# A transformer pair on one core: the spread expert weights are multiplied in on GpSimd instead of VectorE

## Chip, core and metric

One core of one Trainium2 chip. The metric is the device time of one execution, in microseconds (us): the median of several runs. TensorE is the matrix engine (PE; its weight loads are PEld), VectorE is DVE, ScalarE is ACT, GpSimd is POOL, and SyncE (SP) issues nearly all DMAs.

## What is computed

Two transformer layers on x of 4 batches x 512 tokens x 128 features, all float32. Layer 0 is cross attention with 16 heads on a context of 154 rows and a layer of 8 experts of width 512, of which each token uses two. Layer 1 is a masked self attention, a cross attention and a feed-forward with layer norms between them, and then a second expert layer: 32 experts of width 64, of which a router picks six for each token, and a shared expert. This last part is what the change touches. Cut to what matters:

```python
def expert_step(acc, inp):
    gu, dn, c = inp                       # c: this expert's weight for every token
    g = xf @ gu[:I].T
    u = xf @ gu[I:].T
    o = jax.nn.silu(g) * u @ dn.T
    return (acc + c[:, None] * o, None)
routed, _ = jax.lax.scan(expert_step, zeros, (experts_gate_up, experts_down, combine.T))
sh = silu(xf @ shared_gate_w.T) * (xf @ shared_up_w.T)
out = x + routed + sh @ shared_down_w.T
```

The kernel multiplies by c ahead of the down product: (c * silu(g) * u) @ dn, which is the same sum.

## The kernel before

**Tiling.** A batch is one unit of 512 tokens. Features or hidden units lie on the 128 partitions and the 512 tokens on the free axis, so that nearly every instruction of the expert layers is 128x512. In the second expert layer two experts of width 64 fill 128 rows; with the shared expert that makes ND = 17 pairs, n = 0 to 16, n = 0 the shared one. For each pair TensorE makes a gate product into PSUM bank 0 and an up product into bank 1 (`gates`, each by `product3`, three matmuls of split operands, L1493 to L1495), and later a down product (`downs`, L1851, float32, two instructions in the trace), which adds all pairs up in bank 2. Banks 0 and 1 are single: the next gate product waits until ScalarE has read bank 0, the next up product until VectorE has read bank 1.

**Between them** stand, for each pair: ScalarE's silu of bank 0 into `s32` (L1002), VectorE's multiplication of it by bank 1 into one of four buffers of `h32` (L1445, "silu times up"), and for n = 1 to 16 a second VectorE multiplication in place, by a tile of `CB` (L1451). `CB` holds the two experts' weights for all 512 tokens, spread over the 64 partitions of each: the router's weights go to DRAM and come back row by row (`spread_second` on SP, L711, two DMAs for each pair, four slots). A slot is loaded anew when the multiplication that read it is done (`d_h`). A buffer of `h32` is written anew when the down product four pairs before is done (`d_dn`). At the end of a batch ScalarE copies bank 2, TensorE turns it back, VectorE adds it to x (L1459) and SP stores it (L716).

**What else runs beside it.** GpSimd has: for every layer norm an addition (L424) and a power (L427) between VectorE's steps (`Norm`, L395 to L418), the accumulation of the first expert layer (`stage_b`, L776), the addition norm2b (L786), and `split1` (L748), which makes the low half of the second layer's weights out of pieces `raw1`. There are five of these; piece 0 is the shared expert and pieces 1 to 4 serve pairs 1 to 4, 5 to 8, 9 to 12 and 13 to 16. VectorE has the steps of all norms, the attention's maxima and normalisations (L1269 to L1320), the affine steps (L1252, L1255), the split of xT (L1190, L1193) and the router (L1388 to L1431).

**Order.** Every engine works through one list. Each stage is a generator that yields ahead of each step, and `merged` (L75) interleaves the stages of all batches by due times: tables at the head of the file (`PLAN_SP`, `PLAN_POOL`, `PLAN_ACT`, `PLAN_DVE`, `PLAN_PE`) give one number for each step of each batch, and the step with the lowest goes next. The tables come from a planner. On the chip only the order counts: an engine waits for semaphores and for nothing else, and a step that waits holds up all behind it on its engine. The stages overlap over batches: while the second expert layer of batch 0 runs, the attention of batch 3 does, and the router of the next batch runs beside the second expert layer of the one before. Only the second expert layer of batch 3 has nothing beside it.

Of the kernel before, what the change touches and what calls it, by code (L numbers as in the profile page):

```python
# [91 lines left out]
class Signal:  # L92
# [7 lines left out]
    def then(self):  # L100
# [7 lines left out]
    "constants": [[6, 1272, 10975]],  # L108
    "load_x": [[0], [1040], [2704], [5590]],
    "load_context": [[1260], [4711], [7811]],  # L110
    "second_weights": [[14389, 14395, 28061, 38108, 39646, 41268]],
    "load_context1": [[14407], [24876], [31482], [35078]],
    "store": [[48439], [50521], [56182], [57613]],
    "spread_first": [[13617, 13859, 14401, 14945, 15567, 16098, 16858, 17511, 18133], [18975, 19217, 19342, 20142,
        21401, 22143, 23263, 23892, 24870], [26203, 26446, 26452, 27125, 28055, 28944, 30116, 30829, 31476], [32967,
        33210, 33216, 33959, 35072, 35774, 37822, 38062, 38535]],
    "spread_second": [[37816, 38084, 38096, 38541, 38553, 40408, 40666, 41025, 41256, 41444, 41808, 42078, 42388,
# [7 lines left out]
    "norm_a": [[710, 737], [1818, 1845], [3788, 3815], [7460, 7487]],  # L125
    "values": [[1946], [5119], [8117], [11089]],
    "key_tails": [[1983, 3916], [4316, 5058], [8157, 8218], [9729, 11027]],
    "norm_b": [[6000, 6027], [13177, 13204], [18984, 19787], [26163, 26191]],
    "stage_b": [[14945, 15567, 16098, 16858, 17511, 18133, 18858, 19342], [21045, 21401, 22143, 23263, 24803, 24939,
        25480, 26037], [27645, 28055, 28944, 30116, 32053, 32189, 32389, 32873], [34455, 35593, 35774, 36972, 38062,  # L130
        39028, 39269, 40028]],
    "split1": [[24731, 39396, 39671, 40659, 43013]],
    "stage_c": [[19770, 19888, 23766, 23793, 24603, 24630, 25242, 26614, 26642], [26486, 26513, 30945, 30972, 31922,
        31949, 33420, 33790, 33818], [33289, 33316, 36714, 36741, 38426, 38453, 38899, 40154, 40181], [40531, 40558,
        43780, 43807, 45949, 45976, 46745, 48033, 48060]],
    "norm_d": [[30641, 30668], [35461, 35489], [44684, 44712], [49438, 49465]],
# [3 lines left out]
    "split0": [[2783, 3508, 4085, 4134, 4183, 8886, 8935, 8984]],  # L140
    "prepare_a": [[1174], [2939], [5666], [8837]],
    "query_stacks": [[1729, 2105, 2714, 3732], [4391, 5152, 6048, 6659], [7500, 8169, 8735, 9348], [10184, 11142,
        11545, 12352]],
    "key_stacks": [[1500, 1535, 1569, 1604, 1642, 1677, 1778, 1813], [3438, 3473, 4232, 4267, 4904, 4939, 4974, 5009],
        [7143, 7178, 7265, 7300, 7851, 7939, 7974, 8008], [9523, 9558, 9645, 9680, 10873, 10908, 10943, 10978]],
    "group": [[2322, 2429, 2478, 2543, 2593, 2665, 3001], [2890, 3055, 3107, 3259, 3311, 3383, 3634], [3683, 3797,
# [6 lines left out]
    "output": [[5390], [8462], [11308], [14105]],  # L153
    "prepare_b": [[11973, 12537, 13553], [16155, 16980, 18911], [22407, 25236, 26140], [29424, 30188, 32904]],
    "base": [[14692], [20981], [27582], [34392]],
    "gelus": [[13862, 14049, 14159, 14228, 14478, 14633, 14787, 14942, 15100, 15341, 15409, 15611, 15769, 16095, 16207,
# [9 lines left out]
    "stage_c": [[18671, 19695, 20323, 20406, 20426, 20692, 20870, 21031], [27096, 27118, 27139, 27160, 27470, 28555],  # L166
        [33978, 34000, 34021, 34042, 34340, 35280], [40073, 40096, 41062, 41083, 41372, 42859]],
    "exps_c": [[21080, 21246, 21729, 21918], [27694, 27863, 28301, 28489], [34538, 34708, 35353, 35542], [41767, 41939,
        42341, 42529]],
    "moves_c": [[21706, 21983, 22203, 22355], [28604, 29180, 29381, 29514], [35329, 35607, 35827, 36020], [42136,  # L170
        42595, 42820, 43004]],
    "cross": [[22785, 23326, 23495, 23534, 23573, 23932, 25395], [29958, 30331, 30370, 30409, 30448, 30908, 32556],
        [36796, 37218, 37387, 37426, 37465, 37804, 39112], [43715, 44458, 44627, 44666, 44705, 45054, 47035]],
    "prepare_d": [[34947, 36069, 37753], [40444, 41985, 44926], [46139, 46320, 49178], [51071, 51475, 53224]],
# [1766 lines left out]
```

## Time and profile before

| | |
|---|---|
| runs | 597.2 us median of 3 (596.64 to 597.66) |
| profiled execution | 596.67 us, of which the span of the trace is 594.9 us |
| mean granted TensorE clock | 0.997 of full |
| busy, share of the span | PE 96%, PEld 63%, DVE 68%, ACT 54%, POOL 18% |
| first down product of the second expert layer | 415.6 us, last 589.5 us |
| chain that ended last | PE 80%, DVE 10%, ACT 4%, issue 2%, POOL 2% |

A busy PE is modelled from pipelined matmuls, so that 96% busy is not 96% of what the array could do. The granted clock is the share of TensorE's full 2.4 GHz that the chip allowed. The chain of waits goes back from the last instruction, at each step to what released it. "POOL x <- DVE y" in a view of waits reads: GpSimd's instruction that writes x sat waiting for VectorE's that writes y.

### The profile page before, as it was taken

Reading aid. Unit: us, or ns where it says so; the run is one execution under the profiler, and the core shown is the slowest. Engines: PE = TensorE matmul, PEld = TensorE weight load, DVE = VectorE, ACT = ScalarE, POOL = GpSimd, SP = SyncE. Lnnn points to the kernel's source line nnn. Section 1 sums busy time; section 2 is a strip of 40 time slices with the busy share of each in tenths; the row PEclk is TensorE's granted clock in tenths of the full one; section 3 lists DMA queues with packets and bytes.
Section 4 is the critical chain, followed back from the end, with each engine's and each line's share of the span. In section 5 each row is a group of like instructions: output and inputs, shape, how many; then the busy total and the mean of one; then the engine's idle time right before and its main releaser. Section 6 shows DMA issues by size and latency. Waiting matters only on the chain.

```text
span 594.9 us, 8098 instructions
## 1 busy us (share of the span) xinstructions
PE 569.7 (96%) x2512; PEld 374.7 (63%) x2512; DVE 401.7 (68%) x1265; ACT 322.5 (54%) x566; POOL 105.4 (18%) x120
## 2 busy tenths in 40 slices
PE   4899999999999999999999899999899999999997
PEld 3556666665566667656676466666666676666664
DVE  6888989774132344666637585777889999768564
ACT  1587688766454476644855348745292542342321
POOL 3111110000111311242202432126201110100000
PEclk9999999999999999999999999999899999999999
DMA  4400000300311100101111011061321233341431
GB/s 119 195 15 10 18 10 2 105 39 19 107 36 35 54 20 19 36 28 54 60 31 44 14 42 44 1 199 39 122 75 51 90 119 98 111 138 62 143 120 56
DMA packets 23306, 38.35 MB, mean 64 GB/s; under 512 B 3776, under 2 KB 9536, under 8 KB 22880
## 3 DMA queue, kind: packets, MB, share of 16 engines
q1 hardware_dynamic: 22832, 37.44, 19.9%
q8 instruction: 20, 0.33, 0.2%
q10 hardware_dynamic: 432, 0.40, 0.2%
q14 instruction: 22, 0.18, 0.1%
HBM read 36.45 MB, written 1.38 MB: 64 GB/s over the span
## 4 chain that ended last, share of the span: by engine, by line
PE 80%; DVE 10%; ACT 4%; issue 2%; POOL 2%; DMA 1%; DVEq 0%; POOLq 0%; ACTq 0%
PE ps L1681 16%; PE ps L1493 9%; PE ps L1495 9%; PE ps L1851 9%; PE ps L1494 9%; PE ps L1488 3%; PE ps L1568 3%; PE ps L1588 3%; PE ps L1500 3%; PE ps L1603 2%; PE ps L1600 2%; PE ps L1758 1%; PE ps L1738 1%; DVE NM L1156 1%; PE ps L1530 1%
## 5 line engine op out<-in xcount | busy, mean ns | idle before, releaser
L1493 PE MATMUL ps<-xThi,w1s 128*128 128x512 f32 x256 | 147.5, 576 | 2.9 <-DVE h L1445 2.6
L911 ACT ACTIVATE h<-ps,early 128x512 f32<-128x512 f32 x128 | 86.7, 687 | 88.8 <-PE ps L1495 68.9
L1681 PE MATMUL ps<-h,w2s 128*128 128x512 f32 x256 | 122.5, 594 | 3.3 <-DVE ty L1245 3.2
L1495 PE MATMUL ps<-xTlo,w1s 128*128 128x512 f32 x256 | 101.4, 396 | 0.0
L1494 PE MATMUL ps<-xThi,w1s 128*128 128x512 f32 x256 | 100.9, 394 | 0.0
L1002 ACT ACTIVATE s<-ps 128x512 f32<-128x512 f32 x68 | 40.7, 598 | 95.4 <-PE ps L1495 93.8
L1493 PEld LDWEIGHTS ps<-xThi,w1s 128*128 128x128 f32 x256 | 48.5, 190 | 37.3 <-issue 18.2
L1681 PEld LDWEIGHTS ps<-h,w2s 128*128 128x128 f32 x256 | 46.2, 189 | 35.5 <-issue 23.8
L1494 PEld LDWEIGHTS ps<-xThi,w1s 128*128 128x128 f32 x256 | 48.7, 190 | 28.6 <-issue 24.3
L776 POOL TENSOR_TENSOR acc_o<-acc_o,ty 128x512 f32<-128x512 f32 x32 | 41.9, 1310 | 140.2 <-DVE ty L1245 115.7
L1445 DVE TENSOR_TENSOR h<-s,ps 128x512 f32<-128x512 f32 x68 | 46.5, 684 | 28.2 <-PE ps L1495 21.0
L1851 PE MATMUL ps<-h,w2s 128*128 128x512 f32 x128 | 63.5, 592 | 0.0
L1156 DVE TENSOR_REDUCE NM<-ps 128x2 f32<-128x308 f32 x128 | 56.1, 471 | 10.5 <-PE ps L1568 9.2
L1245 DVE TENSOR_TENSOR ty<-ps,WB 128x512 f32<-128x512 f32 x32 | 22.0, 686 | 53.4 <-PE ps L1681 53.4
L1495 PEld LDWEIGHTS ps<-xTlo,w1s 128*128 128x128 f32 x256 | 48.3, 189 | 11.2
L1451 DVE TENSOR_TENSOR h<-h,CB 128x512 f32<-128x512 f32 x64 | 44.2, 690 | 1.0
L1568 PE MATMUL ps<-KS,QS 128*128 128x320 f32 x128 | 41.8, 375 | 2.2 <-DVE NM L1156 1.4
L864 ACT ACTIVATE h<-ps 128x512 f32<-128x512 f32 x54 | 31.1, 597 | 10.8 <-PE ps L1588 9.7
L1568 PEld LDWEIGHTS ps<-KS,QS 128*128 128x128 f32 x128 | 23.6, 194 | 18.4 <-DVE NM L1156 9.7
L1851 PEld LDWEIGHTS ps<-h,w2s 128*128 128x128 f32 x128 | 23.8, 189 | 11.1 <-issue 5.3
L1588 PE MATMUL ps<-QS,KS 128*128 128x512 f32 x64 | 26.2, 440 | 0.4
L798 ACT ACTIVATE QS<-ps 128x512 fp32r<-128x512 f32 x32 | 18.4, 596 | 11.3 <-PE ps L1500 11.0
(264 smaller groups left out, 889.6 us busy)
## 6 DMA issues: line engine op xcount, KB each, us to landing
CB<-ct_rows SPq DMA_DIRECT2D x128, 128.0 KB, 2.9
WB<-wt_rows SPq DMA_DIRECT2D x32, 256.0 KB, 3.2
w2s<-w_dram SPq DMA_DIRECT2D x2, 2048.0 KB, 8.5
raw<-gu_dram SPq DMA_DIRECT2D x4, 512.0 KB, 3.8
x_in<-x_dram SPq DMA_DIRECT2D x4, 256.0 KB, 2.9
w2s<-dn_dram SPq DMA_DIRECT2D x1, 1024.0 KB, 5.7
out_dram<-ty SPq DMA_DIRECT2D x4, 256.0 KB, 2.9
late<-late_dram SPq DMA_DIRECT2D x1, 608.5 KB, 7.5
```

Of the source, the lines that this page charges most:

```text
L776: nc.gpsimd.tensor_tensor(acc_o[:], acc_o[:], ty[:, e % 2, :], ALU.add).then_inc(b_acc.sem, 1)
L911: nc.scalar.activation(h32[:, c % HR, :], bank[c % 2], ACT.Gelu, bias=b1T[:, c:c + 1]).then_inc(b_gelu.sem, 1)
L1156: V.tensor_reduce(NM[:, i, h:h + 2], src, AX.X, ALU.max, negate=True).then_inc(a_nm.sem, 1)
L1445: V.tensor_tensor(h, s32[:, (b * ND + n) % 2, :], bank[1], ALU.mult).then_inc(d_t.sem, 1)
L1451: V.tensor_tensor(h, h, CB[:, slot, :], ALU.mult).then_inc(d_h.sem, 1)
L1493: M(dst, w[0], xThi[:, x, :], start=start, stop=False)
L1494: M(dst, w[1], xThi[:, x, :], start=False, stop=False)
L1495: return M(dst, w[0], xTlo[:, x, :], start=False, stop=stop)
L1568: M(bank[u % 2][:, 0:2 * KW], QS[:, g, i * P:(i + 1) * P], KS[:, g, 2 * half:2 * half + 2, :].rearrange("p h k -> p (h k)"), start=True, s ...
L1588: M(bank[k], lhs, QS[:, g, :], start=True, stop=True).then_inc(a_s_ps.sem, 1)
L1681: M(bank[2], w2s[:, c * P:(c + 1) * P], h32[:, c % HR, :], start=(c % 4 == 0), stop=(c % 4 == 3)).then_inc(b_y.sem, 1)
L1851: M(bank[2], w, h32[:, (b * ND + n) % HR, :], start=(n == 0), stop=(n == ND - 1)).then_inc(d_dn.sem, 1)
```

## The change

1. In VectorE's `stage_d` the multiplication by `CB` is taken out. VectorE keeps silu times up, and one step for each pair where it had two (18 steps for each batch where there were 34).
2. GpSimd gets a stage `weights` of 16 steps for each batch with the same multiplication in place, the same two waits and the same signal `d_h`.
3. All five tables are new, for all stages of all batches. 

```diff
--- PLAN_POOL (new entry; the other entries have new numbers)
+    "weights": [[40900, 41029, 41158, 41287, 41657, 41786, 41917, 42648, 42865, 43214, 43856, 43985, 44481, 44610,
...
+        56754, 56892, 57069, 57292, 57516]],
--- gpsimd
+        def weights(b):
+            for n in range(1, ND):
+                yield
+                h = h32[:, (b * ND + n) % HR, :]
+                pool.wait_ge(d_t.sem, d_t.at(b, n + 1))
+                slot, k = (n - 1) % CR, (n - 1) // CR
+                pool.wait_ge(d_cb[slot].sem, d_cb[slot].at(b, 32 * (k + 1)))
+                nc.gpsimd.tensor_tensor(h, h, CB[:, slot, :], ALU.mult).then_inc(d_h.sem, 1)
+
         every = range(NB)
...
-               ("stage_c", map(stage_c, every)), ("norm_d", [ln_d.gpsimd(pool, b) for b in every]))
+               ("stage_c", map(stage_c, every)), ("norm_d", [ln_d.gpsimd(pool, b) for b in every]),
+               ("weights", map(weights, every)))
--- vector, stage_d
                 V.tensor_tensor(h, s32[:, (b * ND + n) % 2, :], bank[1], ALU.mult).then_inc(d_t.sem, 1)
-                if n:
-                    yield
-                    dve.wait_ge(d_t.sem, d_t.at(b, n + 1))
-                    slot, k = (n - 1) % CR, (n - 1) // CR
-                    dve.wait_ge(d_cb[slot].sem, d_cb[slot].at(b, 32 * (k + 1)))
-                    V.tensor_tensor(h, h, CB[:, slot, :], ALU.mult).then_inc(d_h.sem, 1)
```

The places of the new order that the prediction speaks of, as due times before and after:

| place | before | after |
|---|---|---|
| split1 on GpSimd, pieces 0 to 4 | 24731, 39396, 39671, 40659, 43013 | 35634, 36885, 37831, 41413, 42043 |
| power step of the norm ahead of batch 3's attention, GpSimd | 40558 | 40796 |
| that norm's steps behind it, VectorE | 40665 to 40892 | 41131 to 41317 |
| silu times up of batch 0, pairs 0 to 4, VectorE | 40021, 40214, 40522, 40769, 41019 | 40132, 40473, 40664, 40862, 41144 |
| weights of batch 0, pairs 1 to 7, GpSimd | none | 40900, 41029, 41158, 41287, 41657, 41786, 41917 |
| last up product and the down products behind it, TensorE | 57056; 57124, 57210, 57296 | 57355; 57424, 57510, 57596, 57682 |
| store of batch 2; row 8 of batch 3, SP | 56182, 54830 | 55830, 55836 |
| TensorE between the up and the down product of pair 9, batch 0 | 7 products, 3 downs | 2 products, 2 downs |
| last transposes of batch 2, TensorE | 54261 | 55679 |
| weights of batch 3, pair 9, GpSimd | none | 56340 |

## Rows read from the trace of the kernel before

**Rows 1.** The page, part 1: busy us, share of the span, instructions.
```profile
PE 569.7 (96%) x2512; PEld 374.7 (63%) x2512; DVE 401.7 (68%) x1265; ACT 322.5 (54%) x566; POOL 105.4 (18%) x120
```

**Rows 2.** Windows: length, busy us per engine, PEclk, DMA share, GB/s.
```profile
420.00:440.00 20.00, 18.65 (x71) 13.12 (x72) 17.44 (x48) 11.41 (x21) 0.00 (x0) 0.91 0.31 96
...
460.00:480.00 20.00, 19.54 (x97) 14.22 (x96) 18.26 (x59) 11.59 (x22) 2.88 (x4) 1.00 0.30 96
480.00:500.00 20.00, 20.00 (x77) 13.27 (x77) 19.34 (x69) 6.97 (x12) 2.55 (x3) 1.00 0.34 98
...
560.00:580.00 20.00, 20.00 (x72) 13.36 (x71) 12.94 (x20) 4.83 (x10) 0.00 (x0) 1.00 0.41 122
```

**Rows 3.** Chain that ended last, 403 to 424 us: start, us, what.
```profile
412.86 0.43 DVE h L1445
...
417.49 2.35 DVE ln_c_t L403
...
421.35 0.79 PE ps L1493
```

**Rows 4.** The page, part 5: the multiplication by CB, whole span.
```profile
L1451 DVE TENSOR_TENSOR h<-h,CB 128x512 f32<-128x512 f32 x64 | 44.2, 690 | 1.0
```

**Rows 5.** Groups of instructions on VectorE, 410 to 556 us.
```profile
L1451 DVE TENSOR_TENSOR h<-h,CB 128x512 f32<-128x512 f32 x49 | 33.8, 690 | 0.6
L418 DVE TENSOR_SCALAR normed<-a,ln_n_mv,ln_n_t 128x128 f32<-128x128 f32 x16 | 4.6, 342 | 0.1
...
L1193 DVE TENSOR_TENSOR xTlo<-xT,xThi 128x512 fp32r<-128x512 f32 x3 | 2.1, 684 | 0.0
```

**Rows 6.** Waits, 400 to 560 us: us in total, times, longest.
```profile
PEld ps L1493 <- DVE h L1445: 9.0, 24, 1.8
...
PE ps L1493 <- DVE h L1445: 2.6, 2, 1.7
```

**Rows 7.** Tile CB: issue ns, then us to landing, min/median/max.
```profile
L711 SPq DMA_DIRECT2D CB<-ct_rows x128: 444/595/1676, 390.8 to 580.4; - x128
...
DMA to landing us min/median/max: 2.6/2.9/4.9
```

**Rows 8.** Tiles acc_o, xTlo and h: ns min/median/max, first and last start.
```profile
L776 POOL TENSOR_TENSOR acc_o<-acc_o,ty x32: 1266/1282/1651, 154.4 to 411.2; 128x512 f32<-128x512 f32 x32
...
L1193 DVE TENSOR_TENSOR xTlo<-xT,xThi x8: 656/684/1708, 138.8 to 547.3; 128x512 fp32r<-128x512 f32 x8
...
L1445 DVE TENSOR_TENSOR h<-s,ps x68: 655/686/690, 411.1 to 587.5; 128x512 f32<-128x512 f32 x68
```

**Rows 9.** Timeline, steady part of batch 3: start, us, instruction.
```profile
582.98 0.69 DVE L1445 TENSOR_TENSOR h<-s,ps 128x512 f32<-128x512 f32 x1 [0.84 <-PE ps L1495]
...
584.28 0.39 PE L1493 MATMUL ps<-xThi,w1s 128*128 128x512 f32 x1
...
585.22 0.69 DVE L1445 TENSOR_TENSOR h<-s,ps 128x512 f32<-128x512 f32 x1 [0.82 <-PE ps L1495]
```

**Rows 10.** Chain that ended last, 545 to 595 us.
```profile
560.42 0.86 PE ps L1851 x2
...
590.75 0.67 PE ps L1488 x4
```

**Rows 11.** Timeline at 417 us and at 328 us, GpSimd and VectorE.
```profile
417.43 2.38 POOL L748 TENSOR_TENSOR w1s<-raw,w1s 128x1024 fp32r<-128x1024 f32 x1
417.49 2.34 DVE L403 TENSOR_TENSOR ln_c_t<-ln_c_y 128x4 f32<-128x4 f32 x1 [0.18 <-POOL ln_c_y L427]
...
327.94 2.71 POOL L776 TENSOR_TENSOR acc_o<-acc_o,ty 128x512 f32<-128x512 f32 x2
...
328.00 1.25 DVE L403 TENSOR_TENSOR ln_n_t<-ln_n_y 128x4 f32<-128x4 f32 x1 [1.16 <-POOL ln_n_y L427]
329.29 0.16 DVE L406 TENSOR_TENSOR ln_n_t<-ln_n_t,ln_n_ve 128x4 f32<-128x4 f32 x1
329.48 1.20 DVE L409 TENSOR_SCALAR ln_n_t<-ln_n_t 128x4 f32<-128x4 f32 x1
```

More of the change, by code:

```diff
@@ L107 @@
 PLAN_SP = {
[L108 to L117, printed above, removed]
[4 rows of a table removed]
+    "constants": [[6, 1275, 12533]],
+    "load_x": [[0], [1040], [2568], [4820]],
+    "load_context": [[1263], [4829], [7683]],
+    "second_weights": [[23117, 31807, 36187, 36970, 37135, 38596]],
+    "load_context1": [[16905], [21396], [31813], [36181]],
+    "store": [[47603], [54798], [55830], [57998]],
+    "spread_first": [[13661, 13903, 13909, 14841, 15519, 16187, 16899, 17452, 18119], [19460, 19703, 19709, 20742,
+        21390, 22161, 23111, 23904, 24949], [26962, 27204, 27210, 27648, 28245, 29146, 29980, 30853, 31801], [33045,
+        33287, 33293, 34580, 35244, 36175, 37141, 37705, 38590]],
+    "spread_second": [[38528, 38796, 38808, 38820, 38832, 41036, 41165, 41294, 41423, 41793, 41922, 42053, 42784,
[4 rows of a table added]
 }
@@ L168 @@
[L168 to L173, printed above, removed]
@@ L180 @@
+    "prepare_d": [[34623, 35740, 38465], [41966, 42481, 45334], [45982, 46615, 49587], [50804, 52352, 53609]],
+    "stage_d": [[39768, 40293, 40477, 40707, 40921, 41108, 41417, 41687, 41914, 42302, 42950, 43341, 43502, 43668,
[4 rows of a table added]
 }
 PLAN_DVE = {
[L182 to L184 removed]
@@ L234 @@
-    "feed": [[24402, 24474, 24565, 24737, 24756, 24775, 24858, 24984, 25035, 25098, 25170, 25618, 26025, 26226, 26474,
[6 rows of a table removed]
-    "norm_d": [[29034, 30603, 31105, 31124, 31142, 31227, 33448, 33499], [35333, 35423, 36394, 37351, 38050, 38075,
-        39821, 39872], [43023, 44646, 45058, 45077, 45183, 45208, 45274, 45641], [49310, 49400, 50187, 50206, 50339,
-        50364, 50383, 50786]],
-    "halves_d": [[35295, 37358], [40725, 42756], [47167, 47488], [52481, 53119]],
-    "router": [[36233, 36265, 36296, 36338, 36407, 36434, 36855, 37111, 37180, 37217, 37249, 37281, 37305, 37326],
[3 rows of a table removed]
@@ new lines @@
+    "cross": [[23234, 23299, 23350, 23685, 23705, 24073], [30245, 30296, 30347, 30568, 30609, 31146], [37300, 37338,
+        37389, 38137, 38158, 38415], [44535, 44784, 44842, 45339, 45421, 45746]],
+    "feed": [[24392, 24464, 24555, 24727, 24746, 24765, 24937, 24974, 25054, 25117, 25189, 25718, 25795, 26134, 26206,
[6 rows of a table added]
+    "norm_d": [[28644, 28735, 30438, 30841, 32492, 32516, 32535, 33515], [35377, 35468, 35672, 37122, 37217, 37693,
+        37711, 39219], [41908, 43686, 43859, 44920, 45327, 45352, 45370, 45492], [49323, 49414, 49586, 49605, 50183,
+        50207, 50367, 50418]],
@@ L258 @@
+    "halves_d": [[38478, 39322], [42727, 43998], [46629, 47399], [51227, 51843]],
+    "router": [[36367, 36399, 36430, 36472, 36541, 36898, 36930, 36981, 37128, 37166, 37198, 37814, 37886, 37958],
[3 rows of a table added]
+    "stage_d": [[40132, 40473, 40664, 40862, 41144, 41374, 41619, 41845, 42576, 42793, 43142, 43404, 43571, 43872,
[4 rows of a table added]
 }
 PLAN_PE = {
-    "context_keys": [[720], [1948], [5240], [8257]],
-    "context_values": [[1150], [4648], [7748], [10485]],
-    "inputs": [[1040, 1237], [2576, 3058], [5600, 6147], [8706, 9088]],
@@ L316 @@
-    "prepare_d": [[34476, 35726, 37540], [40381, 40809, 44791], [46070, 46251, 49058], [51002, 51406, 53104]],
-    "gates": [[39496, 39909, 40056, 40125, 40240, 40309, 40424, 40671, 40740, 40853, 40924, 41126, 41194, 41352, 41421,
[8 rows of a table removed]
-    "downs": [[40499, 40585, 41040, 41695, 41781, 41867, 42506, 42592, 42678, 43480, 43566, 44011, 44166, 44389, 44547,
[4 rows of a table removed]
+    "context_keys": [[720], [1825], [5360], [8216]],
+    "context_values": [[1150], [4559], [7618], [10393]],
+    "inputs": [[1040, 1239], [2571, 3039], [5166, 6055], [8143, 8965]],
@@ new lines @@
+    "output": [[5239, 5462], [8338, 8483], [11154, 11397], [13979, 14172]],
+    "prepare_b": [[11276, 11989, 13266], [15430, 16164, 19277], [21940, 23424, 26779], [28024, 28456, 32862]],
+    "first": [[13423, 13748, 14024, 14100, 14354, 14508, 14805, 14873, 15031, 15100, 15473, 15717, 15786, 15941, 16095,
[8 rows of a table added]
+    "weights": [[13890], [20108], [27019], [33871]],
+    "second": [[14268, 14422, 14577, 14663, 14945, 15169, 15255, 15341, 15545, 15631, 15855, 16009, 16257, 16343,
[8 rows of a table added]
+    "stage_c": [[14761, 17673, 19894, 20194, 20395, 20481], [26703, 27108, 27241, 27396], [33726, 34029, 34162, 34316]
+        , [40690, 41400, 41670, 42031]],
@@ new lines @@
+    "scores_c": [[20571, 20731, 21103, 21402], [27626, 27648, 28154, 28370], [34409, 34431, 34902, 35153], [41897,
+        41988, 42282, 42346]],
+    "turns_c": [[21391, 21804, 22073, 22266], [28359, 28548, 29057, 29448], [34970, 35558, 35831, 35953], [42608,
+        42845, 43197, 43370]],
+    "attends_c": [[21829, 22310, 22355, 22422], [29423, 29561, 29606, 29673], [35583, 36083, 36128, 36195], [43554,
+        43717, 43761, 43829]],
+    "cross": [[22821, 23163, 23840, 23953, 24193, 25341, 25612, 26024], [29986, 30173, 30761, 30805, 31444, 32815,
+        33149, 33462], [36422, 37094, 38252, 38295, 38553, 39656, 39785, 40112], [44073, 44346, 45582, 45626, 45913,
+        47319, 47501, 47948]],
@@ L331 @@
+    "prepare_d": [[34546, 35376, 38083], [40904, 42121, 45126], [45729, 46161, 49467], [50740, 52056, 53489]],
+    "gates": [[39587, 40043, 40205, 40320, 40389, 40549, 40618, 40763, 40832, 40947, 41019, 41260, 41329, 41530, 41599,
[8 rows of a table added]
+    "downs": [[40463, 41088, 41174, 41444, 42432, 42519, 42618, 42935, 43021, 43107, 43918, 44185, 44587, 44814, 44900,
[4 rows of a table added]
 }
```

175 lines of the change are left out of this document (80 added, 95 removed), and 177 rows, old and new, of tables (PLAN_ACT, PLAN_DVE, PLAN_PE, PLAN_POOL).

## The prediction

> **What bounds the kernel now.** I read the page's busy line first: TensorE is busy for 96% of the span, VectorE for 68%, GpSimd for 18% [rows 1]. That 96% is modelled, so it doesn't say that nothing can be gained. The windows tell more. In the stretch that the change touches, 416 to 590 us, the second expert layer of batches 0 to 2 runs beside the attention, feed-forward and router of the batches behind it, and there VectorE is nearly full: 17.44, 18.26 and 19.34 us of 20 at 420, 460 and 480, while GpSimd is almost idle [rows 2]. From 556 us the layer of batch 3 runs alone, and VectorE falls to 12.94 of 20. The chain of waits shows what a late VectorE costs: between 412.9 and 421.4 us the end of the kernel hangs on VectorE, 2.35 us of it on one instruction of 4 columns, and TensorE gets its next bank only at 421.35 [rows 3]. Just behind it the granted clock falls: window 420 has a mean of 0.91, so some 3.6 of its 20 us ran at 1.2 GHz instead of 2.4, in the window in which TensorE is idle for 1.35 us [rows 2].
>
> **The order itself** is part of the change. Work on TensorE is the same before and after, instruction for instruction, so its time is that work and the waits between. The due times of the tables are read here as an order only.
>
> **1. The multiplication leaves VectorE.** 64 instructions of 0.690 us, 44.2 us [rows 4], 49 of them (33.8 us) between 410 and 556 us [rows 5]. What can be won is what TensorE waits for VectorE there. Between 400 and 560 us it waits 2.6 us with the array empty for the silu-times-up (L1445), and its weight loads wait 9.0 us for the same, mostly hidden under running matmuls [rows 6]. The slow clock adds 20 x 0.09 = 1.8 us [rows 2]. Bounds: 0 and -11. I take 2.6 + 1.8, rounded to **-4**, since window 480 shows TensorE full although VectorE is at 19.34.
>
> **2. Pieces 1 and 2 of the weight split (L748) go forward** on GpSimd and ScalarE, from the end of the first expert layer of batch 3 (due 39396 and 39671) to its middle (36885 and 37831). Now they fill GpSimd at 404 to 409 us. The piece of the same kind that did show cost 2.35 us [rows 3]. Bounds +1 and -2.4, taken **-1**. The DMAs that feed them go forward too, on SP, where one issue takes about 0.6 us [rows 7].
>
> **3. The multiplication arrives on GpSimd.** Its nearest row is the accumulation acc_o + ty, the same shape and two SBUF inputs: median 1.282, at most 1.651 us [rows 8]. 64 of them are 82 us, so GpSimd goes from 105 to some 188 us, a third of the span. That alone bounds nothing: one expert pair takes TensorE 2.24 us in the steady part (582.98 to 585.22 [rows 9]), against 1.28. Each h comes 0.6 us later (1.282 less 0.690). In the steady part this lies under the four-deep ring of h: in batch 3 the new TensorE order puts four to six other gate and up products and two or three downs between an up product and its own down, 4.5 us and more against 2.2 for both multiplications with their handovers. At the very end three down products (0.86 each [rows 10], 2.6 us) follow the last up product before the last down needs its h, where two did; the same 2.2 us. So the tail costs **0**, and up to +0.6 if that cover is lost.
>
> **4. GpSimd and VectorE shut each other out.** The trace shows it: at 417.49 VectorE's 4-column product, 0.16 us in its sister step at 329.29, lasts 2.34 and ends with the 2.38 us GpSimd instruction that began 0.06 before it. With two GpSimd instructions back to back at 327.94, three VectorE steps take 1.25, 0.16 and 1.20 us [rows 11]. The split of xT, 0.684 us, once takes 1.708 [rows 8]. Silu-times-up reads a PSUM bank and never exceeds 0.690 in 68 executions [rows 8]: it is not shut out itself, but stands in line behind what is. Steps that read only SBUF are therefore the price. The Trainium skill, page "SBUF — State Buffer", section "SBUF: two separate sides", says that the pair of ports is an exclusive lock held for a whole instruction; "Perfetto Trace Analysis", section "Optimizing Scalar/DVE Operations", warns that offloading between the two might not help. By that rule alone the whole of term 1 would be doubtful; the trace agrees on the lock, and no run here shows the offload.
>
> How much: between 410 and 556 us VectorE has some 80 such steps besides L1451, counting a run of four normalisations as one (8 runs of L418, 28 four-column steps of the norms, 8 of the affine, 6 of the split, 21 of the router, 9 others; the longest runs of them are in [rows 5]). 49 multiplications of 1.282 hold the ports for 63 of 146 us, 43%. A step that comes at any time is hit with chance 0.43 and waits 0.64 us on the mean: 34 hits, 22 us. So VectorE is relieved of 33.8 us and given back 22. What of it reaches TensorE: in the steady part silu-times-up ends at 583.67 and the next up product takes its bank at 584.28 [rows 9], a slack of 0.61. Of 34 hits spread evenly over 0 to 1.28, 18 exceed it, by 0.33 on the mean: **+6**. Bounds 0 (VectorE's new idle time takes them all) and +22.
>
> **5. The dense place** is the normalisation before the attention of batch 3, where the 2.35 us were lost. The new order has GpSimd do the power step of that norm (due 40796), then four multiplications, split piece 3, three multiplications and split piece 4 without a break (40900 to 42043), while VectorE has three SBUF-only steps of the feed-forward and five kinds of steps of the norm in a row. The silu-times-ups 1 to 3 come ahead of the norm's steps, so three multiplications are ready: up to 3 x 1.28 = 3.8 us against 2.35 now, and more if the 2.38 us split joins. Bounds -2.3 and +6, taken **+2**: [rows 11] show that back-to-back GpSimd work lets through one or two steps at a time.
>
> **6. GpSimd's small norm steps** queue behind multiplications. Five norms are done in 420 to 550 us; each power step is on a chain to TensorE and finds 0.43 x 0.64 us more: 1.4 us, and one multiplication each at most, 6.4. Behind a waiting multiplication (for its row of CB, or for the silu-times-up) these steps wait too. Taken **+1**.
>
> **7. Rows of CB.** SP loads a row when the multiplication four before is done, now on GpSimd and later by 0.6 us; a row lands 2.9 us after issue (at most 4.9) [rows 7], against four periods of 2.24. Covered. One place is thin: SP's store of batch 2 stands ahead of rows 8 to 12 of batch 3, behind the last transposes of batch 2. From there: 0.67 for the transposes [rows 10], 0.69 for VectorE's sum, 0.6 for the store, 0.6 for the first half row, 2.9, 1.28: 6.8 us, against 8 up and gate products (0.69 each, half of 2.24 less 0.86) and 3 downs, 8.1 us of TensorE work before that h is wanted. With 4.9 it would be 0.7 late. **0**, up to +1.
>
> **8. The rest of the order** (first layer, attention of layer 0) is shuffled by small amounts; waits there are the same kind. **0**, either way 2.
>
> **Sum:** -4 - 1 + 6 + 2 + 1 = +4 on the profiled execution's 596.7, so 600.7. The median of the runs is 597.2, 0.5 above it: **601.2**.
>
> **Rivals.** (B) *VectorE was the limit and is set free.* The hits fall into VectorE's new idle time (some 34 - 22 = 12 us net) and term 5 costs no more than now: -4 - 1, and up to 3 more from the hidden 9.0: 589 to 594, about 592. For it: windows 420 to 480. Against: at 480 TensorE is full beside a VectorE at 19.34, so there is little to free. (C) *The down products wait for GpSimd.* Place: the hand-overs between batches, where power steps, norm2b (L786) and splits hold GpSimd while up to three h are due; each leaves three multiplications, 3.8 us, of backlog, three times: +11, to 608. It decides from the point where the backlog outlasts what TensorE's order puts between; at the narrowest, pair 9 of batch 0, that is two products and two downs, 3.1 us, so a backlog of one multiplication is already too much there. (D) *The two cancel:* relief 4 to 6, hits the same. Measured as no change, which here is within 0.2% (596.0 to 598.4), about what a measurement of this kernel can tell. That the change doesn't do what it says is excluded by the diff: the instruction is removed on one engine and stands on the other.
>
> **Chances.** Forecast 0.52 (598.5 to 605), B 0.26, C 0.10, D 0.12. Slower 0.62, same 0.12, faster 0.26. The range 592 to 607 leaves out half of B and half of C, and takes in the bounds of terms 4 and 5 in part.
>
> **What would show it.** Right: SBUF-only steps of VectorE at 416 to 550 us with means well above those of [rows 5], by 15 to 25 us in all; VectorE's busy time down by clearly less than 44; TensorE idle before L1493 behind L1445 grown, and a slow-clock stretch again at 415 to 430. GpSimd's multiplication at 1.28 to 1.35. Wrong: if those steps keep their means, or keep them long while TensorE's waits shrink (B); if L1851 waits for the GpSimd line (C); if the loss lies ahead of 400 us (term 8).

## The result and the profile after

The changed kernel takes **612.6 us** (median of 4 runs, 607.88 to 613.18) against 596.9 for the kernel before (4 runs, 596.64 to 597.66): ratio 1.0243, 95% interval 1.0217 to 1.0268. It is slower, as forecast, but by 15.7 us instead of 4, which is outside the range. The profiled execution has a span of 611.4 us.

The page of the kernel after has the busy line that answers to [rows 1], and the groups of the two instructions in question (busy us, mean ns of one, idle time ahead of them with its releaser):

```profile
PE 579.4 (95%) x2512; PEld 378.6 (62%) x2512; DVE 380.8 (62%) x1201; ACT 322.4 (53%) x565; POOL 185.5 (30%) x184
...
L797 POOL TENSOR_TENSOR h<-h,CB 128x512 f32<-128x512 f32 x64 | 84.6, 1325 | 77.4 <-DVE h L1456 64.5
...
L1456 DVE TENSOR_TENSOR h<-s,ps 128x512 f32<-128x512 f32 x68 | 46.6, 685 | 56.6 <-PE ps L1500 42.1
```

The 64 multiplications take 1.325 us each on GpSimd, close to the 1.282 of the addition that the forecast took for them. VectorE has lost 44.2 us of work [rows 4], but its busy time fell only from 401.7 [rows 1] to 380.8, by 20.9. So 23.3 us came back to it in steps that last longer. Silu times up, which reads a PSUM bank, did not change: 685 ns.

The windows of the kernel after (busy us of each engine, PEclk, DMA share, GB/s), which answer to [rows 2]:

```profile
380.00:400.00 20.00, 17.96 (x70) 11.42 (x69) 12.75 (x33) 12.50 (x22) 4.86 (x4) 0.91 0.27 82
400.00:420.00 20.00, 20.00 (x86) 13.64 (x86) 16.07 (x47) 8.19 (x15) 10.00 (x10) 1.00 0.14 36
420.00:440.00 20.00, 15.84 (x56) 10.41 (x55) 12.39 (x24) 7.44 (x14) 11.84 (x8) 0.74 0.28 87
...
460.00:480.00 20.00, 18.30 (x82) 11.92 (x81) 17.65 (x59) 10.06 (x22) 6.35 (x6) 1.00 0.12 40
480.00:500.00 20.00, 17.90 (x71) 12.06 (x70) 14.20 (x42) 6.95 (x11) 11.88 (x10) 0.91 0.36 110
500.00:520.00 20.00, 17.75 (x66) 11.18 (x65) 17.36 (x47) 4.16 (x7) 10.82 (x10) 1.00 0.31 94
520.00:540.00 20.00, 19.15 (x75) 12.28 (x74) 12.15 (x28) 6.47 (x12) 10.19 (x9) 1.00 0.31 99
...
560.00:580.00 20.00, 20.00 (x76) 13.39 (x74) 9.03 (x15) 6.28 (x11) 9.98 (x9) 1.00 0.36 112
```

Read PE and PEclk together. TensorE is full in the steady part at the end, as before. It loses most in five windows: 380, 420, 460, 480 and 500. In the first two and at 480 the granted clock is below 1 as well. Each 0.09 of a 20 us window is 3.6 us at 1.2 GHz, 0.26 is 10.4: together 17.6 us at half speed, where the profiled execution of the kernel before had 3.6. That figure varies between executions of one kernel: two others of the kernel before have a mean clock of 0.987, some 15 us at half speed, and took 597.4 and 597.7 us, hardly more than the profiled one.

**Where the time went**, place by place. I gave each matmul its usual start-to-start distance in the trace of before, by tile, and compared the moments at which both profiled executions had done the same sum; the figures are good to about half a microsecond, at 380 to about one. On the time scale of before, the kernel after is 1.4 us ahead at 320, 4.6 ahead at 340 (the kernel before has TensorE idle there for 2.1 us ahead of 333.4), 4.2 ahead at 380, 0.6 behind at 400, 0.3 ahead at 420, 6.0 behind at 440, 10.6 at 480, 16.3 at 520, and 16.5 at 590. So the new order wins some 5 us ahead of 340 and then loses 21: 4.8 at 382 to 394, 6.3 at 420 to 440, 10.7 from 460 to 520, nothing behind.

The waits of the kernel after from 400 us on (us in all, times, longest), which answer to [rows 6]:

```profile
PEld ps L1498 <- DVE h L1456: 19.1, 29, 2.9
POOL h L797 <- DMA CB<-ct_rows: 12.7, 3, 9.1
...
PE ps L1498 <- DVE h L1456: 6.9, 6, 2.1
...
PEld ps L1856 <- POOL h L797: 2.7, 3, 1.6
...
PE ps L1493 <- DVE xi L419: 2.4, 1, 2.4
...
PE ps L1856 <- POOL h L797: 0.7, 1, 0.7
```

TensorE waits for VectorE's silu times up (19.1 us at the weight loads where it had 9.0, 6.9 with the array empty where it had 2.6), not for GpSimd's product (0.7). GpSimd once waits 9.1 us for a row of CB (until 480.33), and TensorE has no stop at that moment.

The dense place, on each engine's timeline of the kernel after (start, us, instruction, idle time ahead): first VectorE, then GpSimd, then TensorE.

```profile
418.07 1.32 DVE L1263 TENSOR_TENSOR gn<-normed,late_rows 128x512 f32<-128x512 f32 x1
419.43 1.65 DVE L1266 TENSOR_TENSOR norm<-gn,late_rows 128x512 f32<-128x512 f32 x1
421.11 1.64 DVE L1363 SCALAR_TENSOR_TENSOR X<-norm,X 128x512 f32<-128x512 f32 x1
...
422.75 0.67 DVE L1456 TENSOR_TENSOR h<-s,ps 128x512 f32<-128x512 f32 x1
...
423.53 1.28 DVE L410 TENSOR_SCALAR ln_c_t<-ln_c_t 128x4 f32<-128x4 f32 x1
424.84 2.27 DVE L413 TENSOR_TENSOR ln_c_t<-ln_c_t,ln_c_y 128x4 f32<-128x4 f32 x1
```

```profile
417.56 4.65 POOL L797 TENSOR_TENSOR h<-h,CB 128x512 f32<-128x512 f32 x3
423.50 1.28 POOL L797 TENSOR_TENSOR h<-h,CB 128x512 f32<-128x512 f32 x1 [1.30 <-DVE h L1456]
424.74 2.35 POOL L749 TENSOR_TENSOR w1s<-raw,w1s 128x1024 fp32r<-128x1024 f32 x1
```

```profile
423.48 0.50 PE L1498 MATMUL ps<-xThi,w1s 128*128 128x512 f32 x1 [1.77 <-DVE h L1456]
...
428.31 1.12 PE L1493 MATMUL ps<-early,xi 128*128 128x128 f32 x4 [2.39 <-DVE xi L419]
```

Three multiplications that GpSimd has in hand alternate with three VectorE steps of 0.69 us, and both sides pay: VectorE's last 1.32, 1.65 and 1.64, GpSimd's three take 4.65 instead of 3.9. Silu times up stands in line behind them, and TensorE stops for 1.77 us. Then two steps of 4 columns take 1.28 and 2.27 us, ending with GpSimd's instructions beside them, and TensorE stops for 2.39 us. The clock falls between the two stops.

The rule that the prediction takes from the Trainium skill, page "SBUF — State Buffer", section "SBUF: two separate sides" (whoever starts first has the port pair for its whole instruction), agrees with these ends.

The stop at 488.66, in the stretch where most is lost, looks the same: two multiplications back to back on GpSimd beside two VectorE steps of 4 columns, which take 0.16 to 0.17 us elsewhere.

```profile
485.26 2.50 POOL L797 TENSOR_TENSOR h<-h,CB 128x512 f32<-128x512 f32 x2
```

```profile
485.32 1.23 DVE L404 TENSOR_TENSOR ln_n_t<-ln_n_y 128x4 f32<-128x4 f32 x1 [1.47 <-POOL ln_n_y L428]
486.59 1.19 DVE L407 TENSOR_TENSOR ln_n_t<-ln_n_t,ln_n_ve 128x4 f32<-128x4 f32 x1
```

```profile
488.66 0.58 PE L1498 MATMUL ps<-xThi,w1s 128*128 128x512 f32 x1 [2.10 <-DVE h L1456]
```

### The profile page after: what moved, and what is told of

Same layout as the page of the kernel before. It is cut to its first block and busy times, and to the rows that moved or that the text cites. A ratio compares the mean times of both kernels' runs of the same rounds, so it can differ in the third digit from the quotient of the medians.

```text
span 611.4 us, 8097 instructions
## 1 busy us (share of the span) xinstructions
PE 579.4 (95%) x2512; PEld 378.6 (62%) x2512; DVE 380.8 (62%) x1201; ACT 322.4 (53%) x565; POOL 185.5 (30%) x184
## 3 DMA queue, kind: packets, MB, share of 16 engines
q1 hardware_dynamic: 22832, 37.44, 19.1%
## 5 line engine op out<-in xcount | busy, mean ns | idle before, releaser
L1686 PE MATMUL ps<-h,w2s 128*128 128x512 f32 x256 | 123.3, 597 | 1.5 <-DVE ty L1256 1.5
L797 POOL TENSOR_TENSOR h<-h,CB 128x512 f32<-128x512 f32 x64 | 84.6, 1325 | 77.4 <-DVE h L1456 64.5
L1856 PE MATMUL ps<-h,w2s 128*128 128x512 f32 x128 | 64.9, 606 | 0.7 <-POOL h L797 0.7
L1256 DVE TENSOR_TENSOR ty<-ps,WB 128x512 f32<-128x512 f32 x32 | 22.1, 690 | 55.6 <-PE ps L1686 52.0
L1573 PE MATMUL ps<-KS,QS 128*128 128x320 f32 x128 | 43.2, 393 | 1.5 <-DVE NM L1167 0.7
L1856 PEld LDWEIGHTS ps<-h,w2s 128*128 128x128 f32 x128 | 24.3, 194 | 13.1 <-issue 6.3
## 6 DMA issues: line engine op xcount, KB each, us to landing
late<-late_dram SPq DMA_DIRECT2D x1, 608.5 KB, 7.5
```

The source lines that it names most:

```text
L797: nc.gpsimd.tensor_tensor(h, h, CB[:, slot, :], ALU.mult).then_inc(d_h.sem, 1)
L1573: M(bank[u % 2][:, 0:2 * KW], QS[:, g, i * P:(i + 1) * P], KS[:, g, 2 * half:2 * half + 2, :].rearrange("p h k -> p (h k)"), start=True, s ...
L1686: M(bank[2], w2s[:, c * P:(c + 1) * P], h32[:, c % HR, :], start=(c % 4 == 0), stop=(c % 4 == 3)).then_inc(b_y.sem, 1)
L1856: M(bank[2], w, h32[:, (b * ND + n) % HR, :], start=(n == 0), stop=(n == ND - 1)).then_inc(d_dn.sem, 1)
```

## The experiments

All ratios are to the kernel before, run on the same chip beside them; its median there was 597.6 to 598.0 us. The 95% intervals reach 1.0 to 2.6 us to either side, so a difference of less than about 2 us between two experiments says nothing. The table holds the main outcome, medians in us. "Hybrid" is the new order up to due time 35000 (about 355 us of the run: the GpSimd steps of the kernel after that are due at 34580 and 35244 start at 349.7 and 356.3) and the old one behind it. The two parts are called the early and the late order.

| on the engines | old order | hybrid | new order |
|---|---|---|---|
| multiplication on VectorE | 597.6 (before) | 590.7 | 608.7 |
| multiplication on GpSimd | 602.4 | 596.2 | 612.6 (after) |
| multiplication left out, power on 4 columns on GpSimd | 594.4 | 586.3 | 593.6 |

**Engine or order?** The new order with the multiplication back on VectorE, directly behind silu times up:

```diff
-               ("weights", map(weights, every)))
...
+                if n:
...
+                    V.tensor_tensor(h, h, CB[:, slot, :], ALU.mult).then_inc(d_h.sem, 1)
```

> The new order of all engines, but the multiplication by CB back on VectorE, directly behind silu times up; GpSimd has none. Theory L (GpSimd's multiplications hold the SBUF ports that VectorE's SBUF-only steps need; TensorE idles behind them and its clock falls): 594 to 600 us, the sum of the blocked time on VectorE back to about 21 us, at most 4 us of slow clock. Theory O (the new order is the worse one, whoever multiplies): 607 us or more.

608.7 us, ratio 1.0188 (1.0144 to 1.0231): theory O's time, and not theory L's. Some 4 us of it are this kernel's own: at 580 to 586 us, where the order has the store of batch 2 ahead of a row of CB, VectorE waits 3.81 us for that row and TensorE 2.23 us for VectorE. Without that it would be near 605, an estimate. The new order is slow with either engine, so this run alone does not divide the loss.

The old order with the multiplication on GpSimd, at the due times at which VectorE had it:

```diff
-                    V.tensor_tensor(h, h, CB[:, slot, :], ALU.mult).then_inc(d_h.sem, 1)
+                nc.gpsimd.tensor_tensor(h, h, CB[:, slot, :], ALU.mult).then_inc(d_h.sem, 1)
```

> The old order, and only the engine changed: GpSimd multiplies at the due times that VectorE's multiplication had. Theory L: 604 to 616 us, with steps of VectorE of 1.2 us and more where they took 0.16 to 0.7. Theory O: 595 to 599 us.

602.4 us, ratio 1.0078 (1.0047 to 1.0109), between the two theories' ranges. The move between engines costs 4.8 us by itself in the old order, near the 4 that the prediction's sum gave for the whole change.

**GpSimd's time or its long SBUF instruction?** In both orders the multiplication is left out and GpSimd executes a power on 4 columns in its place, which lasts nearly as long, waits for the same and gives the same signal (these kernels leave out the weights, so their result is not the layer's):

```diff
-                nc.gpsimd.tensor_tensor(h, h, CB[:, slot, :], ALU.mult).then_inc(d_h.sem, 1)
+                nc.gpsimd.tensor_tensor(scrap[:, at:at + NT], two[:], mhalf[:], ALU.pow).then_inc(d_h.sem, 1)
```

> The changed kernel with the multiplication by CB left out: GpSimd instead runs, at the same places behind the same waits, a power of 4 columns (1.04 us in the trace, against 1.29), which touches the ports for next to nothing. Theory L: 592 to 598 us. Rival P (what costs is the later h, a hop over a third engine, not the ports): 608 us or more, since the hop and 1.04 of 1.29 us stay. Theory O: 607 us or more.

> The old order with GpSimd multiplying, but the multiplication left out and the 4-column power of 1.04 us in its place. Theory L: 590 to 596 us, that is 7 to 12 us under the 602.4 of the same order with the multiplication. If the two stretches of order are equally sensitive, the difference is the 19 us that the new order showed (612.6 less 593.6); if the new order is the more sensitive, it is well under that.

593.6 us (ratio 0.9932, 0.9909 to 0.9955) in the new order and 594.4 (0.995, 0.9931 to 0.997) in the old. Both are in theory L's ranges. The group of the power in the new order, and the busy lines of both pages, new order first:

```profile
L801 POOL TENSOR_TENSOR scrap<-two,mhalf 128x4 f32<-128x4 f32 x64 | 66.3, 1040 | 77.8 <-DVE h L1460 62.9 <-DMA CB<-ct_rows 14.8
...
PE 568.8 (96%) x2512; PEld 375.5 (63%) x2512; DVE 358.7 (61%) x1201; ACT 322.4 (54%) x565; POOL 167.4 (28%) x185
```

```profile
PE 568.4 (96%) x2512; PEld 373.9 (63%) x2512; DVE 360.1 (61%) x1201; ACT 322.7 (55%) x566; POOL 171.4 (29%) x185
```

and of the old order with the multiplication on GpSimd (e2):

```profile
PE 573.5 (96%) x2512; PEld 375.0 (62%) x2512; DVE 383.6 (64%) x1201; ACT 322.9 (54%) x566; POOL 189.0 (31%) x184
```

Read the DVE figure. The same 1201 instructions take 380.8 us beside the multiplication and 358.7 beside the power in the new order: 22.1 us of being held up. In the old order it is 383.6 less 360.1, 23.5 us. The amount is the same. What it costs is not: 612.6 less 593.6 is **19.0 us** in the new order, 602.4 less 594.4 is **8.0** in the old. (The power is also 0.28 us shorter than the multiplication, which these differences include.)

**Where the order turns from gain to loss.** The kernel before, multiplication on VectorE, in the hybrid order:

> The kernel before, its multiplication on VectorE, with the new order only up to due time 35000 and the old order behind. The changed kernel was 4.8 us ahead of the one before at 340 to 380 us of its trace. If that lead is the new order's own and stands by itself: 592 to 595 us, faster than both. If it hangs on what follows: 596 to 600 us.

590.7 us, ratio 0.9876 (0.9854 to 0.9898), below both ranges. In its profile a lead of 5.8 us stands at 340 and is kept to the end. So the early order is worth 6 to 7 us by itself, and the late one is what loses.

The hybrid order with the multiplication on GpSimd, and with the power in its place (multiplication left out):

> The order of e9_hybrid_order (590.65 us) with the multiplication on GpSimd instead of on VectorE, which is the engine swap of the change without the later part of its order. Theory A (prices add: the swap costs 4.8 us in the old order, where its steps stand, and this part of the order is the old one): about 595.5, range 594 to 598. Theory B (the swap costs what it costs with the new order, 612.6 against 608.7, less): 593 to 595. Theory C (what the change loses lies in the engine swap and is as large in any order, 15 us or more): above 603.

> The kernel of e12_hybrid_pool (596.23 us) with the multiplication left out and the power on 4 columns in its place on GpSimd, as in e6_power_in_place. With it both late orders have been run with both instructions on GpSimd. Theory A (the late part of the new order costs nothing by itself and nearly all of its loss comes from GpSimd's long SBUF instructions): near the 593.56 of e6_power_in_place or a few us below, 588 to 591, so that the long instructions cost 5 to 8 us with the old late order against 19.0 with the new one. Theory B (the late part of the new order is itself slow by about 16 us, whatever GpSimd executes): near 577 to 580, with the long instructions costing 16 to 19 us here too. Theory C (in the hybrid order the power leaves waits that the multiplication also has, because they come from VectorE's own steps): 594 to 596.

596.2 us (ratio 0.9967, 0.995 to 0.9984) and 586.3 (0.9816, 0.9787 to 0.9845). Their busy lines, in this order:

```profile
PE 571.4 (96%) x2512; PEld 375.3 (63%) x2512; DVE 380.0 (64%) x1201; ACT 323.4 (54%) x566; POOL 186.1 (31%) x184
```

```profile
PE 566.3 (97%) x2512; PEld 373.8 (64%) x2512; DVE 355.7 (61%) x1201; ACT 323.0 (55%) x566; POOL 167.8 (29%) x185
```

VectorE is held up for 24.3 us, again the same, and it costs 9.9 us. The swap costs 5.5 us, as in the old order and as theory A had it. The late order costs 16.4 us with the multiplication on GpSimd (612.6 less 596.2), 18.0 with it on VectorE (608.7 less 590.7, some 4 of them the wait for a row of CB), and 7.3 with the power (593.6 less 586.3). So 7.3 are lost by this order even where VectorE is left alone, and the rest appears where VectorE is late, whether GpSimd's long instructions or its own multiplications make it so. Neither theory A nor B of the last expectation is met in full: it came out 1.7 us below A's band, and the order's own share is 7.3 where A said nothing and B 16.

**Where each of them loses.** The comparison by TensorE's work done, made for these kernels too, in us behind the profiled execution of the kernel before (minus is ahead; the moments are those of the kernel before):

| kernel | at 340 | 340 to 400 | 400 to 440 | 440 to 520 | 520 to 590 | at 590 |
|---|---|---|---|---|---|---|
| new order, GpSimd (after) | -4.6 | +5.1 | +5.2 | +10.7 | +0.1 | +16.5 |
| new order, VectorE | -5.7 | +5.1 | +1.7 | +7.1 | +4.2 | +12.4 |
| new order, power | -6.0 | +5.1 | -1.4 | -0.5 | -0.4 | -3.1 |
| hybrid, GpSimd | -5.7 | +0.1 | +2.6 | +1.4 | +0.9 | -0.7 |
| hybrid, power | -6.7 | +0.1 | -3.0 | -1.1 | +0.1 | -10.7 |
| old order, GpSimd | +1.0 | 0.0 | +2.7 | +1.0 | +0.9 | +5.5 |

GpSimd's first multiplication comes at 417 us, and the 5.1 us at 340 to 400 are lost in all three kernels of the new order: they belong to the order and not to the change of engine. Behind 400 us the kernel with GpSimd's multiplications loses 16.0 us in the new order, and 4.9 and 4.5 with the old late order. (The +1.0 of the last row at 340 is a slow clock behind a stop at 333 us: window 320 to 340 is at 0.91 there, at 1.00 in the kernel before.)

**Single places.** In the kernel after, piece 2 of the weight split, which stands at 384 us, is held until VectorE has normalised the weights of batch 2's cross attention (`PN2`, L1330 there):

```diff
                 yield
+                if k == 2:
+                    pool.wait_ge(c_pn2.sem, c_pn2.at(2, 2))
```

> The kernel after, but the split piece of batch 2 that the new order puts at 384 us on GpSimd waits until its attention's second product is done, as late as before. Theory A (this piece, alternating with the 1.28 us additions of GpSimd, holds up the small steps and the routing weights at 382 to 394 us, and TensorE waits 2.0 us for them and then goes 3.4 us at the slow clock): about 4 us come back, 612.6 to about 608.5, the idle time before the use of the routing weights near 389 us is gone. Theory B (the place is late for another reason, the order of VectorE's own steps): within 1 us of 612.6, the idle time stays. Theory C (the piece only moves into a dense stretch behind): 611 to 614, with the idle time gone at 389 and a new one at 395 to 410.

608.2 us, ratio 1.0172 (1.014 to 1.0204): 4.4 us come back, as theory A had it. The kernel after at that place, on VectorE, GpSimd and TensorE:

```profile
382.94 3.65 DVE L419 TENSOR_SCALAR xn<-X,ln_d_mv,ln_d_t 128x128 f32<-128x128 f32 x2
...
388.47 0.28 DVE L1442 SCALAR_TENSOR_TENSOR cw<-tw,tr 128x128 f32<-128x128 f32 x1
```

```profile
382.92 1.28 POOL L777 TENSOR_TENSOR acc_o<-acc_o,ty 128x512 f32<-128x512 f32 x1 [3.86 <-DVE ty L1256]
384.15 2.36 POOL L749 TENSOR_TENSOR w1s<-raw,w1s 128x1024 fp32r<-128x1024 f32 x1
```

```profile
388.81 0.61 PE L1822 MATMUL ps<-early,cw 128*32 128x128 f32 x4 [2.04 <-DVE cw L1442]
```

and VectorE with the piece held back:

```profile
382.33 1.59 DVE L419 TENSOR_SCALAR xn<-X,ln_d_mv,ln_d_t 128x128 f32<-128x128 f32 x2
...
385.80 0.28 DVE L1444 SCALAR_TENSOR_TENSOR cw<-tw,tr 128x128 f32<-128x128 f32 x1
```

Two normalisations that take 3.65 us behind the addition and the piece take 1.59 behind the addition alone. The routing weights `cw` come 2.1 us earlier, counted from the start of these normalisations, and the stop of 2.04 us and the slow clock behind it are gone. With the power in place of the multiplication the new order has the same stop, which confirms that it is the order's:

```profile
387.47 0.61 PE L1826 MATMUL ps<-early,cw 128*32 128x128 f32 x4 [2.05 <-DVE cw L1446]
```

In the kernel after, GpSimd's first multiplication waits until the norm ahead of the attention of batch 3 is finished:

```diff
+                if b == 0 and n == 1:
+                    pool.wait_ge(ln_c.out.sem, ln_c.out.at(NB - 1, NT))
```

> The changed kernel, but GpSimd waits ahead of its first multiplication of batch 0 until the normalisation ahead of batch 3's attention is written. Theory L: the stretch 417 to 434 us loses its blocked steps (some 6 us of VectorE) and most of its 10 us of slow clock: 603 to 608 us. Rival (the down products wait for GpSimd): no gain or a loss, 612 to 616 us.

608.5 us, ratio 1.0173 (1.0135 to 1.0212): 4.1 us back, half a microsecond outside theory L's range. VectorE of this kernel, and then TensorE:

```profile
417.21 0.68 DVE L1265 TENSOR_TENSOR gn<-normed,late_rows 128x512 f32<-128x512 f32 x1
417.93 0.69 DVE L1268 TENSOR_TENSOR norm<-gn,late_rows 128x512 f32<-128x512 f32 x1
418.66 0.69 DVE L1365 SCALAR_TENSOR_TENSOR X<-norm,X 128x512 f32<-128x512 f32 x1
...
427.51 0.69 DVE L1458 TENSOR_TENSOR h<-s,ps 128x512 f32<-128x512 f32 x1 [5.87 <-PE ps L1502]
```

```profile
423.04 3.65 PE L1858 MATMUL ps<-h,w2s 128*128 128x512 f32 x4 [4.01 <-POOL h L799]
```

The three steps are back at 0.69 us, but the products held back are then late for TensorE: it stops for 4.01 us ahead of a down product, which is what rival C describes, and VectorE has nothing to do for 5.87 us because no up product comes. By the comparison of work done this kernel loses 2.7 us at 400 to 440 where the kernel after loses 5.2.

Each multiplication of the kernel after cut in two of 256 columns, so that VectorE can come in between:

```diff
-                nc.gpsimd.tensor_tensor(h, h, CB[:, slot, :], ALU.mult).then_inc(d_h.sem, 1)
+                for c in (slice(0, 256), slice(256, 512)):
+                    last = nc.gpsimd.tensor_tensor(h[:, c], h[:, c], CB[:, slot, c], ALU.mult)
+                last.then_inc(d_h.sem, 1)
```

> The changed kernel, each GpSimd multiplication cut into two of 256 columns (some 0.7 us each, 1.45 for both). Theory L: the ports are free once in the middle, so a blocked step of VectorE waits 0.35 us on the mean and not 0.64: 603 to 609 us, though GpSimd works longer. Rival P (the later h costs): 613 us or more.

```profile
PE 573.4 (95%) x2512; PEld 375.9 (62%) x2512; DVE 375.2 (62%) x1201; ACT 322.4 (53%) x565; POOL 196.8 (33%) x248
...
L798 POOL TENSOR_TENSOR h<-h,CB 128x256 f32<-128x256 f32 x128 | 95.9, 773 | 63.8 <-DVE h L1458 50.4 <-DMA CB<-ct_rows 13.2
```

606.6 us, ratio 1.0155 (1.0131 to 1.0178): 6.0 us back, although GpSimd works 11 us more, in theory L's range. VectorE's busy time is 375.2, so it is held up for 16.5 us (less 358.7) instead of 22.1: a quarter less, not half.

**The slow clock.** Five matmuls whose results nobody reads, in TensorE's two stops at 420 to 430 (two ahead of the up product of pair 5 of batch 0, three ahead of the attention of batch 3):

> The changed kernel with five more TensorE matmuls of 0.86 us each on constants, into a free bank, where TensorE idles: two ahead of the up product of pair 5 of batch 0, three ahead of the transposes of batch 3's attention. If the slow clock of 424 to 434 us comes from that idling, it goes, and 3 to 5 us with it: 608 to 610 us. If the clock falls anyway, 612 to 616 us.

```profile
420.00:440.00 20.00, 19.33 (x76) 12.18 (x75) 14.15 (x36) 11.62 (x18) 11.07 (x7) 1.00 0.23 76
```

609.0 us, ratio 1.0192 (1.017 to 1.0214), in the range for a clock that falls because of the idling. In the profiled execution window 420 goes from 0.74 to 1.00, and 3.6 us come back in the median. By the comparison of work done the stretch 400 to 440 loses 2.3 us where the kernel after loses 5.2, so of the 6.3 us at 420 to 440 some 3 are the clock's and the rest the stops themselves. The mean granted clock goes from 0.986 to 0.997; a part of that is window 480, which is at 1.00 here too, though no filler stands there.

**A faster version.** The hybrid order, multiplication on VectorE, with piece 3 of the weight split (the fourth of five, which meets the norm ahead of batch 3's attention) held until that norm is finished:

```diff
+                if k == 3:
+                    pool.wait_ge(ln_c.out.sem, ln_c.out.at(NB - 1, NT))
```

> The order of e9_hybrid_order (590.65 us: the new order up to due time 35000, the old one behind it, multiplication on VectorE), with the last batch's split piece on GpSimd held until the norm of its batch is finished. Theory A (that piece's 2.35 us keep the norm steps of VectorE waiting at 411 to 415 us, and this is what stops TensorE there and brings the slow clock): 587 to 589.5, no stretch at the slow clock near 415 us. Theory B (the product of expert weights stops for other steps there): 590 to 591.5, the same idle time.

The step that costs 2.35 us in [rows 3], in the hybrid order without and then with the hold:

```profile
411.72 2.34 DVE L268 TENSOR_TENSOR ln_c_t<-ln_c_y 128x4 f32<-128x4 f32 x1 [0.18 <-POOL ln_c_y L292]
```

```profile
412.18 0.17 DVE L268 TENSOR_TENSOR ln_c_t<-ln_c_y 128x4 f32<-128x4 f32 x1 [0.18 <-POOL ln_c_y L292]
...
410.00:420.00 10.00, 9.42 (x41) 6.25 (x39) 9.68 (x30) 4.81 (x9) 4.04 (x3) 1.00 0.26 80
```

**588.8 us**, ratio 0.9849 (0.983 to 0.9868), in theory A's range, and the fastest kernel of this study that computes everything: 1.5% below the kernel before, with one wait more and the early order, and no change of engine. The granted clock at 410 to 420 is 1.00 where it was 0.83 without the hold. Nearly all of the gain is the early order's; the 1.9 us that the hold adds are at the edge of what the intervals tell apart.

## Why the prediction was right or wrong

The direction was right, and the mechanism too: VectorE and GpSimd shut each other out, and more of that reached TensorE than the relief was worth. What failed is the step from held-up time on VectorE to time of the kernel, for the order that was being forecast. The swap of engines alone costs 4.8 us in the old order, 5.5 in the hybrid and 3.9 in the new one (some 8 there, if the wait for a row of CB is taken out of the kernel with the multiplication on VectorE), near the sum's +4 in the first two. The other 10 to 11 us of the 15.7 come only together with the new late order, in which a late VectorE costs far more. By its own terms:

- **Term 4, how much** VectorE is held up, was right: 22 us forecast from 34 hits, 22.1 to 24.3 measured in three orders. **What of it reaches TensorE was mis-sized**, and this is the step that failed. The forecast laid the hits evenly over time and took from each the slack of 0.61 us of the steady part of batch 3 in the old order: +6, with +2 for the dense place (term 5) and +1 for the small steps (term 6), +9 in all. The long instructions cost 8.0 and 9.9 us with the old late order, where the +9 holds, and **19.0 us** with the new one. The +22 at the upper end of term 4 held it; the value taken was near the lower one. At the two places read above the hits do not come one at a time: VectorE's SBUF-only steps stand in chains, two or three multiplications are ready beside them, and the chain is lengthened by 2.5 us at 418 (three steps of 0.69 us take 4.61) and by 2.1 us at 485, where the slack was taken as 0.61.
- **Term 5** named the place and the mechanism (three multiplications ready against VectorE's steps in a row), +2 with a bound of +6; the profile shows 6.3 at 420 to 440. It left out the slow clock behind longer stops: 10.4 us at half speed at this place, and the run with the fillers gave some 3 us back. Term 1 had counted on that clock to rise.
- **Term 2 had the wrong sign.** The pieces that are brought forward do not only leave their old place, they arrive at a new one. There piece 2 holds two normalisations and the routing weights, and holding it back gains 4.4 us. The forecast compared it with idle time on GpSimd and did not look at what VectorE does beside it.
- **Term 8 was not zero:** the early order gains 6.9 us (597.6 less 590.7; 5.8 in the profile), far outside its +-2. With the 5.1 us lost at 340 to 400 it comes to nearly nothing, and so does the forecast's -1 for terms 2 and 8. That agreement is luck: two errors of some 6 us cancel. Of the 15.7 us, then, nearly all arose behind 400 us.
- **Term 1** can be read with the old late order, where the power in place of the multiplication relieves VectorE with almost nothing in return: 597.6 less 594.4, 3.2 us, and in the hybrid 590.7 less 586.3, 4.4, against 4 forecast. Right there. In the new order the same step is worth 15.1 (608.7 less 593.6, some 4 of them the wait for a row of CB): in this order TensorE hangs on VectorE far more, whatever makes VectorE late.
- **Terms 3 and 7 were right** for the kernel after: no loss in the steady part behind 520, and no stop of TensorE for rows of CB. The thin place that term 7 names showed up with the multiplication back on VectorE, where it cost some 4 us. Term 6 was not separated.
- **Rival C** (down products wait for GpSimd) had its share: 0.7 us with the array empty and 2.7 at weight loads. **Rival B** would have been 592; what it describes is seen where the port is not held (593.6, new order, multiplication left out).

The profiles add up: some 5 us won early (4.6 in the kernel after, 5.8 in the hybrid), 4.8 lost at 382 to 394, 6.3 at 420 to 440, 10.7 at 460 to 520. The last of these has no experiment of its own. The profile shows it as stops behind silu times up (1.26 us ahead of 467.21, 2.10 ahead of 488.66, 1.11 ahead of 516.85) with lengthened SBUF steps ahead of them at the one place shown, and it is gone with the power in place (TensorE is full there, 20.00 of 20 in window 480). How it divides over the single norms stays open. So does what in the new late order takes the slack away: that it does so is measured, by 15.1 and 19.0 us against 3.2 to 4.4 and 8.0 to 9.9, but no run changes single steps of it behind 440 us.

## What to carry to other kernels

Before SBUF-only work moves to GpSimd, line up both engines' instructions in the stretches where VectorE has chains of SBUF-only steps that TensorE waits for; the total of held-up time says little, since the same 22 to 24 us cost 8 us in one order and 19 in another. Take the slack from the order that will run, and at the chains, not from a steady part of the old order. When an instruction is moved, price its new place as well as its old one, and when an order is new throughout, test its early and late part separately: here one was worth 7 us and the other cost more than twice that. Where the move must be made, shorter instructions on GpSimd (6.0 us) or one wait in front of the instruction that meets the chain (4.1 and 4.4 us) each took back a quarter to two fifths of the 15.7 us; together they were not run.

## What was not expected of the hardware

- Alternating on the port pair slows both: GpSimd's multiplication went from 1.28 to 1.55 us on the mean of three beside VectorE steps that went from 0.69 to 1.32, 1.65 and 1.64.
- An instruction of 1.04 us on GpSimd that reads 4 columns leaves VectorE all but alone, while one of 0.77 us on 256 columns does not (VectorE busy for 375.2 us beside 128 of these, 358.7 beside 64 powers): what costs is GpSimd's reading and writing of many columns, not its being busy. Leaving VectorE alone is read from its busy time, 22 to 24 us lower over the same 1201 instructions than beside the whole multiplications.
- A stop of 2.04 us was followed by 3.6 us at the lower of the clock's two levels, and one of 1.77 us by 10.4 us, in which a stop of 2.39 us lies; with five matmuls in those two stops window 420 stayed at 1.00, and 3.6 us came back. A stop of this length does not always bring the clock down: ahead of 333 us TensorE stops for 2.13 us in the kernel before and for 2.11 and 2.13 us in the two other kernels of the old order, and window 320 to 340 has a mean clock of 1.00 in the first and 0.91 in the others.
